# Two attention layers on one core: in layer 1, one tile of every four is turned by DMA instead of by TensorE

## The reference

```python
# layer 0
Bm, Cm, Dm = Wb @ xf, Wc @ xf, Wd @ xf                 # per image, (256, 1024)
S = softmax(einsum('bcn,bcm->bnm', Bm, Cm), axis=-1)   # (1024, 1024)
x = gamma * einsum('bcm,bnm->bcn', Dm, S) + x
# layer 1: group norm (32 groups), then 4 heads of 64 channels
hn = group_norm(x)
q, k, v = wq @ hn + bq, wk @ hn + bk, wv @ hn + bv
attn = softmax(einsum('bhdq,bhdk->bhqk', q, k) * 64 ** -0.5, axis=-1)
out  = einsum('bhqk,bhdk->bhdq', attn, v)
x = x + (wp @ out + bp)
```

## Time and profile before

| | |
|---|---|
| time, median of 3 runs | 682.79 us (682.38 to 683.4) |
| profiled execution, its own time | 682.95 us |
| its span in the profile | 681.0 us |
| granted TensorE clock | 1.00 throughout |
| layer 1 in the span | from about 243 us to the end |
| busy shares | TensorE 98%, VectorE 82%, ScalarE 67%, GpSimd 34% |

### The profile page before, as it was taken

How to read it: one execution, slowest core, us unless ns; L and a number is a source line. 1 busy time by engine, 2 the same in 40 slices (tenths; PEclk the granted TensorE clock), 3 DMA queues, 4 the chain that set the end, 5 groups by cost and what they waited for, 6 DMA issues and landing times.

```text
span 681.0 us, 11125 instructions
## 1 busy us (share of the span) xinstructions
PE 668.9 (98%) x3668; PEld 568.5 (83%) x3668; DVE 560.4 (82%) x910; ACT 455.7 (67%) x790; POOL 231.2 (34%) x216
## 2 busy tenths in 40 slices
PE   8989999999999899999999999999999999999997
PEld 7878888888888778888888888888888888988886
DVE  4787768768678478998888899888899888889996
ACT  5563435435435167988787788777789778778884
POOL 0130211201125024565233465242546433334531
PEclk9999999999999999999999999999999999999999
DMA  7476856645645957001656010367110265301001
GB/s 227 85 134 188 170 99 138 155 100 128 165 97 123 213 141 203 1 1 48 146 119 185 17 47 1 93 155 193 54 54 8 58 157 126 92 16 47 1 32 62
DMA packets 96714, 69.50 MB, mean 102 GB/s; under 512 B 71072, under 2 KB 73376, under 8 KB 96672
## 3 DMA queue, kind: packets, MB, share of 16 engines
q1 hardware_dynamic: 96672, 68.97, 41.8%
HBM read 18.62 MB, written 8.39 MB: 40 GB/s over the span
## 4 chain that ended last, share of the span: by engine, by line
PE 86%; DVE 5%; issue 3%; ACT 2%; POOL 2%; DMA 1%; SPq 1%; POOLq 0%; DVEq 0%; ACTq 0%
PE acc L1410 36%; PE scores L1410 26%; PE trans L1444 16%; PE trans L1410 8%; DVE negmax L979 1%; ACT prob L739 1%; DMA x_raw<-in_x 1%; POOL planes L638 1%; DVE pt_lo L997 1%; ACT pt_hi L749 1%; DVE pt_lo L1168 1%; DMA turned<-planes 0%; POOL y_in L649 0%; SPq L466 0%; DVE qk L1132 0%
## 5 line engine op out<-in xcount | busy, mean ns | idle before, releaser
L626 POOL TENSOR_SCALAR prob<-prob,rsum 128x1024 f32<-128x1024 f32 x127 | 142.8, 1124 | 256.7 <-DVE rsum L984 256.7
L739 ACT ACTIVATE prob<-scores,negmax 128x1024 f32<-128x1024 f32 x160 | 178.9, 1118 | 74.4 <-DVE negmax L979 72.9
L979 DVE TENSOR_REDUCE negmax<-scores 128x1 f32<-128x1024 f32 x160 | 194.0, 1213 | 17.8 <-PE scores L1410 16.6
L749 ACT ACTIVATE pt_hi<-trans 128x512 fp32r<-128x512 f32 x256 | 139.6, 594 | 63.9 <-PE trans L1444 63.3
L997 DVE TENSOR_TENSOR pt_lo<-trans,pt_hi 128x512 fp32r<-128x512 f32 x256 | 163.5, 680 | 1.0 <-ACT pt_hi L749 0.6
L1410 PE MATMUL scores<-k_st,q_st 128*128 128x512 f32 x512 | 137.9, 391 | 0.7 <-issue 0.7
L1444 PEld LDWEIGHTS trans<-ident,prob 128*128 128x128 f32 x1024 | 117.7, 140 | 22.5 <-issue 4.2
L1444 PE MATMUL trans<-ident,prob 128*128 128x128 f32 x1024 | 134.6, 273 | 1.2 <-DVE pt_lo L997 1.1
L1410 PEld LDWEIGHTS scores<-k_st,q_st 128*128 128x128 f32 x512 | 95.7, 188 | 21.6 <-issue 1.2
L1410 PE MATMUL acc<-pt_hi,v_st 128*128 128x512 f32 (+1 forms) x264 | 106.8, 407 | 0.6 <-DVE pt_lo L997 0.6
L1410 PE MATMUL acc<-pt_lo,v_st 128*128 128x512 f32 (+1 forms) x264 | 101.0, 385 | 0.0
(11 more groups left out here) (163 smaller groups left out, 1028.0 us busy)
## 6 DMA issues: line engine op xcount, KB each, us to landing
k_st<-qk SPq DMA_DIRECT2D x64, 256.0 KB, 4.7
q_st<-qk SPq DMA_DIRECT2D x64, 128.0 KB, 2.4
x_raw<-in_x SPq DMA_DIRECT2D x8, 512.0 KB, 5.2
y_out<-in_x SPq DMA_DIRECT2D x16, 256.0 KB, 3.3
y_scratch<-y_out SPq DMA_DIRECT2D x16, 256.0 KB, 2.3
y_in<-y_scratch SPq DMA_DIRECT2D x4, 1024.0 KB, 7.5
y_res<-y_scratch SPq DMA_DIRECT2D x16, 256.0 KB, 3.7
out<-y_res SPq DMA_DIRECT2D x14, 256.0 KB, 2.1
```

The source lines that it names most:

```text
L626: nc.gpsimd.tensor_scalar(p, p, rsum[:, t % 2:t % 2 + 1], 1.0, ALU.mult, ALU.mult)\
L739: nc.scalar.activation(prob[:, t % 2, :], scores[:, t % 2, :], ACT.Exp, bias=negmax[:, t % 2:t % 2 + 1], scale=1.0, accum_out=rowsum[:, t ...
L749: nc.scalar.activation(pt_block(pt_hi, (t // 4) % 2, t, h), trans[:, h, :].rearrange("p (j n) -> p j n", n=P), ACT.Copy).then_inc(pt_high, 1)
L979: nc.vector.tensor_reduce(negmax[:, t % 2:t % 2 + 1], scores[:, t % 2, :], AX_X, ALU.max, negate=True).then_inc(max_ready, 1)
```

## The change

Tiles 0, 4, 8, ... of each image of layer 1 (not tile 28 of the last image) are turned by DMA, 31 tiles in all. The other 97 stay as they were. For a turned tile:

- `exp` writes into a buffer of its own, `prob_turned` (the memory of `planes[:, 1]`), with a third column in `rowsum` and `rsum`.
- VectorE makes a scaled reciprocal; GpSimd's multiplication writes the float16 high plane in place of `normalise`.
- TensorE's eight transposes go away, and so do `trans_high` and `trans_low`.
- VectorE writes the low plane in step s, where `trans_low` stood.
- SyncE issues two DMA transposes, at step s of its new, unrolled program. The restack or store of a group of step s - 1 stands behind the two transposes of step s. The second residual load moves from an image's end to the start of the next image's program.
- ScalarE widens the high plane in step s + 1, behind `exp` of tile s + 3 and ahead of the copies of that step's groups.
- GpSimd widens the low plane in step s + 2, behind the normalisation of tile s + 3.

```diff
+def is_turned(i, s):
+    last_half = isinstance(i, int) and i == IMAGES - 1 and s >= T1_IMAGE - 4
+    return s % 4 == 0 and not last_half
...
+        prob_turned = flat(planes[:, 1, :, :].bitcast(F32))
...
+            def turn1_high(i, s):
+                d = turned_before(i, s)
+                slot = d % 2
+                sp.wait_ge(prob_ready, T1_BASE + T1_IMAGE * i + s + 1)
+                if d < 2:
+                    sp.wait_ge(pt_split, SPLIT_CREDIT + TILES_LAYER0 - 1 + d)
+                else:
+                    sp.wait_ge(turned_split, d - 1)
+                sp.dma_start_transpose(turned[slot][:, 0, :, :], planes[:, 0, 0, :]).then_inc(turned_hi[slot], 16)
+
+            def turn1_low(i, s):
+                d = turned_before(i, s)
+                slot = d % 2
+                sp.wait_ge(low_plane, PLANE_CREDIT + TILES_LAYER0 + d + 1)
+                sp.dma_start_transpose(turned[slot][:, 1, :, :], planes[:, 0, 1, :]).then_inc(turned_lo[slot], 16)
...
             def image1(i):
                 plan = plan1(i)
...
                 if not plan.first:
...
+                    load_residual(i - 1, 1)
+                for s in range(T1_IMAGE):
+                    if is_turned(i, s):
+                        turn1_high(i, s)
+                        turn1_low(i, s)
+                    if s == 3 and not plan.last:
+                        sp.wait_ge(h_split, 4 * i + 4)
+                        load_y(i + 1)
+                    if s == 15:
+                        load_residual(i, 0)
+                    for name in ends(STEPS1[s - 1]) if s > 0 else []:
...
+                if plan.has("next_qk6"):
+                    restack(plan, "next_qk6")
...
+            def high_plane1(i, s):
...
+                nc.gpsimd.tensor_scalar(planes[:, 0, 0, :], prob_turned, rsum[:, 2:3], PROB_SCALE,
+                                        ALU.mult, ALU.mult).then_inc(prob_ready, 1)
...
+            def turned_low1(i, s):
+
+                slot = turned_before(0, s) % 2
+                pool.wait_ge(pt_high, high_number(i, s))
+                wait_scalar(turned_lo[slot], turns1(i, s))
+                nc.gpsimd.tensor_scalar(pt_tile(pt_lo, s), turned[slot][:, 1, :, :], 1.0 / PROB_SCALE, 1.0,
+                                        ALU.mult, ALU.mult).then_inc(turned_split, 1)
...
+                    if not is_turned(i, s):
+                        trans_high(i, s, before)
+                    if s + LAG < T1_IMAGE:
+                        exp1(i, s + LAG)
+                    elif not plan.last:
+                        exp1(i + 1, s + LAG - T1_IMAGE)
+                    if s % 4 == 1 and is_turned(i, s - 1):
+                        turned_high1(i, s - 1)
...
+            def plane_low1(i, s):
...
+                nc.vector.scalar_tensor_tensor(planes[:, 0, 1, :], prob_turned, rscaled[:, 0:1], planes[:, 0, 0, :],
+                                               ALU.mult, ALU.subtract).then_inc(low_plane, 1)
...
                 if part == 0:
...
+                    pe.wait_ge(pt_split, SPLIT_CREDIT + splits_before(i, 4 * (j + 1)))
+                    pe.wait_ge(turned_split, turned_before(i, 4 * (j + 1)))
```

More of the change, by code:

```diff
@@ L707, in image1 @@
                 for s in range(T1_IMAGE):
-                    if s + 1 < T1_IMAGE - DVE_TILES or not plan.last:
-                        normalise(T1_BASE + T1_IMAGE * i, s + 1)
+                    if s + 1 < T1_IMAGE:
+                        if s + 1 < T1_IMAGE - DVE_TILES or not plan.last:
+                            normalised(i, s + 1)
+                    elif not plan.last:
+                        normalised(i + 1, 0)
+                    if s >= 2 and is_turned(i, s - 2):
+                        turned_low1(i, s - 2)
                     if plan.first and s == GN_STEP + SUM_BEHIND:
@@ L949, in image1 @@
                         evacuate(plan, head_outputs(STEPS1[s]), i)
-                    trans_high(t1, s, before)
-                    if s + LAG < T1_IMAGE or not plan.last:
-                        exp(t1, s + LAG)
+                    if not is_turned(i, s):
+                        trans_high(i, s, before)
+                    if s + LAG < T1_IMAGE:
+                        exp1(i, s + LAG)
+                    elif not plan.last:
+                        exp1(i + 1, s + LAG - T1_IMAGE)
+                    if s % 4 == 1 and is_turned(i, s - 1):
+                        turned_high1(i, s - 1)
                     if not plan.last and s - 1 in NORM_STEPS1:
@@ L1354, in image1 @@
                 for s in range(T1_IMAGE):
+                    if s + 1 < T1_IMAGE:
+                        recip1(i, s + 1)
+                    elif not plan.last:
+                        recip1(i + 1, 0)
                     if s + 1 < T1_IMAGE or not plan.last:
-                        recip(t1, s + 1)
+                        if (s + 1) % 4 == 0 and is_turned(i, (s + 1) % T1_IMAGE):
+                            scaled_reciprocal1(*((i, s + 1) if s + 1 < T1_IMAGE else (i + 1, 0)))
                         if plan.last and s + 1 >= T1_IMAGE - DVE_TILES:
```

165 lines of the change are left out of this document (112 added, 53 removed).

## The result

The changed kernel takes 727.17 us (median of 4 runs, 725.9 to 729.8), the kernel before 682.84 us beside it (682.38 to 683.4). The ratio is 1.065, 95% interval 1.0626 to 1.0674: slower, as forecast, but by 44.3 us, where 17.1 were forecast and 26 were the range's end.

A forecast was written before the change was run, and what follows sets the result against it. Long blocks were taken as bound by TensorE, 15 others by VectorE; -6.3 + 10.2 + 9.9 + 3.3 = +17.1 us on 682.95 us gave 700.0 us. The range was 681 to 709 us.

The forecast's parts named there:

- the costs of each new instruction: Per turned tile: VectorE's 1.28 us becomes 1.30 and 0.15 us (+0.17 us), ScalarE's 1.08 us becomes 1.06 us.
- ScalarE's waits at the three image starts: Sign in the profile: ScalarE's high-plane widening idle some 4 us for a DMA at the last three images' starts.
- blocks of VectorE nearly full: In blocks without three projection groups VectorE has little slack: busy for 10.67 us of one of 10.99 us.
- GpSimd's low widening: GpSimd's widening of the low plane was costed at nothing; over 2.5 us long it would delay normalisation and transposes.
- The ordinary long block: TensorE-bound blocks 5 to 7 of the first three images: each gains 0.7 us, -6.3 us for nine.
- The image start: Blocks 0 and 1 of the last three images: ScalarE waits for tile 0's late high plane, +9.9 us in all.
- The first image's tile 4: Its high transpose stands behind the 1 MB load of y_in; ScalarE waits 3.5 us, costing +3.3 us.
- The VectorE-bound blocks: 15 blocks: +0.17 us VectorE work and exp 0.8 us late, mean +0.68 us each, +10.2 us in all.
- Rival 2: Image starts stall, but ScalarE's place does no harm in ordinary blocks: 690 us, chance 0.2.
- rival 1: Stalls are absorbed, TensorE-bound blocks gain 0.8 us each, and the kernel is faster: 672 us, chance 0.15.
- 3: ScalarE's place harms, but tile 0's transposes overtake the loads and are in time: 683.5 us, chance 0.07.
- Rival 4: Transposes slower among k copies; other widenings (tile 28) wait too, some 3 us in three images: 709 us or more, chance 0.06.

## Why the prediction was wrong

**Right:** slower; the costs of each new instruction; ScalarE's waits at the three image starts and at one place of the first image; blocks of VectorE nearly full; GpSimd's low widening well under the 2.5 us at which it was to cost (1.05 us). That it costs nothing at all is not shown: weight loads for the transposes waited for a normalisation 4.8 us in all, 1.0 us at most.

**The ordinary long block, forecast -0.7 us each, measured +0.96 (8.62 / 9). This step failed.** It compared sums: TensorE's 14.2 us of work against VectorE's 14.4 to 14.6. It read the shift of the widening only where VectorE waits for `exp`, in the short block. It did not ask for the long block what is queued behind the widening on ScalarE, which is the copy of a group, and who waits for that: VectorE, and TensorE through its bank. The measured block has 0.95 us of the 1.06 us widening on the path, as the chain above shows, and TensorE waits 0.44 to 1.25 us in each for a part of `qk`. With the widening behind the copy it is 14.09 us (126.78 / 9), 0.01 from before. So the gain that the sums promised did not come either: within the block TensorE waits for VectorE, VectorE for ScalarE and ScalarE for VectorE, and only when VectorE had 0.93 us less did 0.55 us of TensorE's saving appear.

**The image start, forecast +3.3 us each, measured +8.4 (25.15 / 3). The mechanism was named, its path to TensorE was not.** The step let ScalarE's delay reach TensorE at tile 3's transposes, which stood at 473.84 before: 477.1 for 473.8. But TensorE needed VectorE's part of `qk7` for the group that it began at 470.7 before (by the chain), 3.1 us ahead of those transposes. By the step's own 475.3 that is 4.6 us; it became gaps of 6.19, 5.12 and 5.82 us. Two more terms were off: the transpose lands after 5.07, 3.97 and 4.58 us at the three starts, where the step had 4.05 (472.8 less 468.75), and TensorE's clock falls after each gap, which the step did not have at all and which costs up to 2.4 us. At the third image's start, the one that the step worked out, the two blocks grew by 7.1 us, with a gap of 5.12 us. At the second image's start gap and clock are 8.6 us together, of the 9.4 us by which its two blocks grew (the split was not tried by itself). And what holds the transpose was put on the wrong transfers: the residual loads by the step, the k copies by the run.

**The first image's tile 4, +3.3 forecast, +4.5 measured.** ScalarE's wait was 3.48 us, as forecast (3.5); the rest, 1 us, went when the widening's place was changed (16.45 us).

**The VectorE-bound blocks, +0.68 us forecast, +0.40 measured (6.01 / 15).** In block 4 it is 11.51 for 10.82 us. Of the 0.8 us by which `exp` was to be late, VectorE shows 0.15 + 0.29 us of waits; the rest of 0.25 us is the low plane, the scaled reciprocal and seams, forecast at 0.17. Why the waits are 0.44 and not 0.8 us was not tried. A version without ScalarE's widening lost them; in this block VectorE lost as much again beside GpSimd, in the kind as a whole 1.9 us were won.

**The rivals.** Rival 2 (ScalarE's place does no harm) and rival 1 are refuted, as is 3. Rival 4 named the k copies' traffic, but where it puts the harm, at tile 28, 0.4 us is to be seen, once (the five waits are 5.3, 4.3 and 4.9 us at the three starts, 3.5 at tile 4 and this one). The range ended 26 us above before because no case had TensorE stop at its accumulation bank.

## What to carry to other kernels

When an instruction that waits for a transfer is put into an engine's queue, list what stands behind it up to the accumulation bank: a late copy that should empty a bank stops TensorE, as it did here, whatever the busy shares say. Where engines with nearly equal work wait for one another in a loop, relieving one may give nothing back, as here; take work from the others too, or measure first with another's part cut short, as the run with the short low plane does. A transfer that is waited for goes ahead of the bulk ones in its queue, not right behind them; and what goes behind it then comes later too, as `y_in` and the k copies showed.

## What the runs showed of the hardware

- **The clock after a gap.** After gaps of 6.19 and 5.62 us TensorE went on at its lower level: granted clock 0.58 over 376 to 384 us in the changed kernel, matmuls of 256 columns 0.41 us for 0.28. It fell after less, too: with the widening behind the copies TensorE was idle for 2.54 us and did eight transposes from 372.59, and the granted clock was 0.50 from 373.8 to 380.6 us. After an idle time of 1.28 us, with the transposes first, it stayed at 1.00 (463 to 470 us). With the transposes first the mean granted clock of the run is 0.998, in the changed kernel 0.984.
- **A transpose behind k copies.** At the second image's start it landed 3.1 us after issue with none of them ahead, 6.98 us right behind four of them, 5.07 us behind these and two residual loads; in the first image 8.29 us behind the 1 MB load. Issuing it 2.5 us earlier into the same traffic brought 0.6 us. Of the 62 transposes of a whole plane in layer 1 of the changed kernel 42 landed 3.0 to 3.2 us after issue, the others after up to 8.6; in layer 0 it was 3.0 to 4.4 us.
- **VectorE beside GpSimd.** The low plane took 1.27 or 1.28 us with no pass of GpSimd beside it, 1.34 to 1.37 when GpSimd's normalisation covered its first 0.27 to 0.30 us, 1.41 to 1.43 at 0.34 to 0.36 us, and 1.79 and 1.80 at 0.71 and 0.73 us. The Trainium skill, page "SBUF — State Buffer", "Who interferes with whom", says that a VectorE instruction with two SBUF inputs contends with a GpSimd instruction that reads SBUF, and that the contention is an exclusive lock. The trace agrees in kind: VectorE's instruction, always the second here, lengthens by the overlap less some 0.2 us.
- **GpSimd's two-input pass** over 128 x 1024 took 2.15 us in 31 cases, where a one-input pass takes 1.13.
